# Row maxima handed over in two halves in both self-attentions, with the first pass of layer 0 begun earlier in the ring

## The reference

```
layer 0:  q, k, v = per-head layernorm(x @ W + b)
          scores = einsum('bqhd,bkhd->bhqk', q, k) * 16 ** -0.5
          probs  = softmax(scores, axis=-1)
          out    = einsum('bhqk,bkhd->bqhd', probs, v) @ Wo + bo
layer 1:  the same on q, k, v = x @ qkv_w + qkv_b, with a causal mask before the softmax
```

## Time and profile before

| | |
|---|---|
| median of 3 runs | 1895.42 us |
| profiled execution, time / span | 1903.1 / 1901.4 us |
| busy in the span: PE, DVE, ACT, POOL | 1543.4, 1226.4, 941.4, 515.6 us |
| mean granted clock of TensorE | 0.91 |
| L1113 (row maxima), 448 times | 481.2 us busy, 1107 ns each |
| L1045 (exponentials), 896 times | 440.1 us busy |
| L954, L993, L1005 on PE | 286.4, 272.4, 220.8 us busy |
| layer 0's attention, first fill to last output turned | 118.3 to 562.9 us |
| layer 1's first fill | 1132.1 us |

### The profile page before, as it was taken

How to read it: one execution, slowest core, us unless ns; L and a number is a source line. 1 busy time by engine, 2 the same in 40 slices (tenths; PEclk the granted TensorE clock), 3 DMA queues, 4 the chain that set the end, 5 groups by cost and what they waited for, 6 DMA issues and landing times. The chain is left out here.

```text
span 1901.4 us, 27565 instructions
## 1 busy us (share of the span) xinstructions
PE 1543.4 (81%) x8891; PEld 836.8 (44%) x8892; DVE 1226.4 (64%) x4679; ACT 941.4 (50%) x1856; POOL 515.6 (27%) x419
## 2 busy tenths in 40 slices
PE   5858999999973688888877767999987883369997
PEld 3511222222222566666666533333326672136664
DVE  6978887877505999999992446777725567501211
ACT  2823777777663555555544432666673652111211
POOL 1791000000001466555553150111211332240111
PEclk9956999999897899999987876999998996679999
DMA  6293334221010000000000186355402122531110
GB/s 210 82 210 58 45 47 99 41 41 18 26 32 13 1 2 1 1 1 1 1 2 1 34 232 89 46 69 111 90 3 88 15 40 36 202 106 36 45 45 8
DMA packets 112679, 106.01 MB, mean 56 GB/s; under 512 B 45523, under 2 KB 86555, under 8 KB 112542
## 3 DMA queue, kind: packets, MB, share of 16 engines
q1 hardware_dynamic: 107281, 93.83, 23.4%
q0 software_dynamic: 2640, 6.31, 0.9%
q10 hardware_dynamic: 2624, 4.19, 0.7%
HBM read 68.56 MB, written 36.41 MB: 55 GB/s over the span
## 5 line engine op out<-in xcount | busy, mean ns | idle before, releaser
L1113 DVE TENSOR_REDUCE arena<-banks 128x2 f32<-128x1024 f32 (+1 forms) x448 | 481.2, 1107 | 162.2 <-PE banks L954 105.6
L1045 ACT ACTIVATE arena<-banks 128x512 f32<-128x512 f32 (+3 forms) x896 | 440.1, 557 | 188.1 <-PE banks L993 181.5
L954 PE MATMUL banks<-arena 96*128 96x512 bf16 (+3 forms) x896 | 286.4, 397 | 55.3 <-DMA arena<-v 26.8
L993 PE MATMUL banks<-arena 98*128 98x512 bf16 (+3 forms) x896 | 272.4, 364 | 9.3 <-ACT arena L1045 6.8
L1005 PE MATMUL banks<-arena 128*32 128x512 f32 (+3 forms) x1792 | 220.8, 565 | 12.6 <-ACT arena L1045 6.5
L1712 DVE MATCH_REPLACE8 arena<-arena 128x77 f32<-128x77 f32 x1024 | 213.8, 223 | 0.0
L954 PEld LDWEIGHTS banks<-arena 96*128 96x128 bf16 x896 | 80.8, 102 | 238.3 <-DVE arena L1113 137.7
L993 PEld LDWEIGHTS banks<-arena 98*128 98x128 bf16 x896 | 82.5, 98 | 188.5 <-ACT arena L1045 124.4
L1602 POOL TENSOR_SCALAR arena<-arena 128x256 f32<-128x256 f32 x32 | 39.2, 1224 | 449.8 <-DVE arena L1689 449.8
L2498 DVE COPY arena<-banks 128x1024 f32<-128x1024 f32 x23 | 28.2, 1225 | 198.6 <-PE banks L2432 198.6
L1704 DVE MAX8 arena<-arena 128x8 f32<-128x77 f32 x1024 | 149.5, 224 | 0.9
(11 more groups left out here) (279 smaller groups left out, 2465.3 us busy)
## 6 DMA issues: line engine op xcount, KB each, us to landing
arena<-parts SPq DMA_DIRECT2D x192, 128.0 KB, 7.4
parts<-arena SPq DMA_DIRECT2D x24, 512.0 KB, 5.3
arena<-in_L_ffn_W SPq DMA_DIRECT2D x12, 1024.0 KB, 10.9
v<-arena SPq DMA_DIRECT2D x32, 256.0 KB, 2.3
arena<-v SPq DMA_DIRECT2D x16, 512.0 KB, 11.1
arena<-in_L_ffn_W ACTq DMA_DIRECT2D x4, 1024.0 KB, 9.4
arena<-sorted_rows SPq DMA_DIRECT2D x23, 129.0 KB, 2.2
arena<-sorted SPq DMA_DIRECT2D x23, 128.0 KB, 2.1
```

The source lines that it names most:

```text
L954: mm = pe.matmul(bank[:, 0:w], qst[r][0:KS, j, i * P:(i + 1) * P], kst[r][0:KS, j, kb * BANK:kb * BANK + w], start=True, stop=not diag)
L993: pe.matmul(bank, kst[r][0:KM, j, kt * P:(kt + 1) * P], qst[r][0:KM, j, half * BANK + lo:(half + 1) * BANK], start=True, stop=True).then_i ...
L1045: act.activation(prob[:, gi % 2 * G + j, lo:BANK], PS[:, 4 + n % 3, 0:BANK - lo], ACT.Exp, scale=SCALE).then_inc(sem(s + "_exp"), 1)
L1113: dve.tensor_reduce(m2[u % 2][:, 2 * pair:2 * pair + 2, i, kb], PS[:, 2 * (n % 2):2 * (n % 2) + 2, 0:w], AX.X, ALU.max).then_inc(sem(s + " ...
```

## The change

The maxima of a unit are handed over in two halves of 512 queries. DVE's three steps, PE's transpose, DVE's copy and the DMA now exist per half: 128x16 numbers each (32 rows after the transpose), and four DMAs, one per head, instead of one. Buffers `mh`, `mx` and `mT` are now indexed by the half, no longer by the unit's parity. PE's pass waits for the first half's rows at its start (`_rows0`) and for the second half's before the first group of the second half (`_rows1`).

The entries stand in the ring as follows: MAX of half 0 four fills after the last fill of that half, MAX of half 1 where MAX stood. In layer 0 (`not causal`) the deadlines also move: 24 fills instead of 40 come before the first pass, pass u carries the entries up to fill 28 of unit u+1, and in the passes of units 0 and 7 the entries up to that unit's second MAX are spread over the first quarter (`goal`, `early`). Layer 1 keeps its deadlines.

On SP, unit 2 is no longer loaded straight after unit 1: its 13 DMAs are issued after the row DMAs of unit 0. The waits of the following stages count one more ring entry per unit.

```diff
@@ -856,7 +856,7 @@
             R.at = SMALL_AT + SPARE
             m2 = [R.f32(G * TB * 2).rearrange("p (j t a) -> p j t a", j=G, a=2) for _ in range(2)]
             mx = [R.f32(G * TB).rearrange("p (j t) -> p j t", j=G) for _ in range(2)]
-            mh = [R.bf16(2 * G * TB) for _ in range(2)]
+            mh = [R.bf16(G * TB) for _ in range(2)]
             mT = [R.bf16(P) for _ in range(2)]
             rs = [R.f32(TB * G // 2).rearrange("p (t j) -> p t j", j=G) for _ in range(2)]
             osb = [out_area[:, half * BANK:(half + 1) * BANK] for half in range(2)]
@@ -867,8 +867,11 @@
             diagonal = [gi for gi, (half, kt, lo) in enumerate(groups) if causal and kt * P >= half * BANK]
             last_of = [max(i for i, g in enumerate(groups) if g[0] == half) for half in range(2)]
 
-            def hilo(u):
-                return mh[u % 2].rearrange("p (c j t) -> p c j t", c=2, j=G)
+            HT = TB // 2
+            HALF_FILLS = sum(1 for f in unit_fills if f[0] < HT)
+
+            def hilo(half):
+                return mh[half].rearrange("p (j c t) -> p c j t", c=2, j=G)
 
             PV_AT = G - 1 if causal else 1
             OUT_AT = G - 1 if causal else 2
@@ -877,11 +880,24 @@
             for u in range(NU):
                 feed += [(FILL, u, f) for f in range(NF)]
             for u in range(NU):
-                feed.insert(feed.index((FILL, u, NF - 1)) + (5 if u < NU - 1 else 1), (MAX, u, 0))
+                feed.insert(feed.index((FILL, u, HALF_FILLS - 1)) + 5, (MAX, u, 0))
+                feed.insert(feed.index((FILL, u, NF - 1)) + (5 if u < NU - 1 else 1), (MAX, u, 1))
+            first_due = feed.index((FILL, 1, AHEAD) if causal else (FILL, 0, 24))
             due = []
             for u in range(NU):
-                due.append(feed.index((FILL, u + 2, AHEAD)) if u + 2 < NU else len(feed))
-            first_due = feed.index((FILL, 1, AHEAD))
+                n, f = (u + 2, AHEAD) if causal else (u + 1, NF - 4)
+                due.append(feed.index((FILL, n, f)) if n < NU else len(feed))
+            early = 0.25
+
+            def goal(u, past):
+
+                at0 = due[u - 1] if u else first_due
+                if u in (0, NU - 1) and not causal:
+                    soon = max(at0, feed.index((MAX, u, 1)) + 1)
+                    if past <= early:
+                        return at0 + round((soon - at0) * past / early)
+                    return soon + round((due[u] - soon) * (past - early) / (1 - early))
+                return at0 + round((due[u] - at0) * past)
 
             def width(gi):
                 return BANK - groups[gi][2]
@@ -896,9 +912,9 @@
                 for gi in range(NGR):
                     for j in range(G):
                         past += width(gi) / G
-                        goal = at0 + round((due[u] - at0) * past / WORK)
-                        ring += feed[at:goal]
-                        at = goal
+                        upon = goal(u, past / WORK)
+                        ring += feed[at:upon]
+                        at = upon
                         if j == 2 and gi in (1, last_of[0] + 2):
                             half = 0 if gi > 1 else 1
                             if u or gi > 1:
@@ -913,14 +929,18 @@
             @block.sync
             def _(sp):
                 sp.wait_ge(sem(q + "_parts"), PARTS_ST)
-                for u in range(1, NST):
-                    load_unit(sp, l, u)
+                load_unit(sp, l, 1)
                 sp.wait_ge(sem(s + "_ones"), NST)
                 for u in range(NU):
 
-                    sp.wait_ge(sem(s + "_red"), entry[MAX, u, 0] + 1)
-                    sp.dma_start(qst[u % NST][KS:KM], mT[u % 2][0:2 * G * TB]).then_inc(sem(s + "_rows"), 16)
-                    if 1 <= u <= NU - NST:
+                    for half in range(2):
+                        sp.wait_ge(sem(s + "_red"), entry[MAX, u, half] + 1)
+                        for j in range(G):
+                            sp.dma_start(qst[u % NST][KS:KM, j, half * BANK:(half + 1) * BANK], mT[half][j * 2 * HT:(j + 1) * 2 * HT]
+                                         ).then_inc(sem(f"{s}_rows{half}"), 16)
+                    if u == 0:
+                        load_unit(sp, l, 2)
+                    elif u <= NU - NST:
                         sp.wait_ge(sem(s + "_pv"), u * NGR)
                         load_unit(sp, l, u - 1 + NST)
                     if l == 0 and u == 2:
@@ -957,9 +977,9 @@
                             mm = pe.matmul(bank[:, w - P:w], identb, future, start=False, stop=True)
                     mm.then_inc(sem(s + "_fill"), 1)
 
-                def turn_maxima(n, u):
-                    pe.wait_ge(sem(s + "_mh"), u + 1)
-                    pe.transpose(PS[0:2 * G * TB, 2 * (n % 2), 0:P // 2].bitcast(BF16), mh[u % 2], identb
+                def turn_maxima(n, u, half):
+                    pe.wait_ge(sem(s + "_mh"), 2 * u + half + 1)
+                    pe.transpose(PS[0:G * TB, 2 * (n % 2), 0:P // 2].bitcast(BF16), mh[half], identb
                                  ).then_inc(sem(s + "_fill"), 1)
 
                 def turn_output(n, u, half):
...
@@ -1013,8 +1033,11 @@
                 if l == 0:
                     pe.wait_ge(sem("xv"), 2 * B)
                 for u in range(NU):
-                    pe.wait_ge(sem(s + "_rows"), 16 * (u + 1))
+                    pe.wait_ge(sem(s + "_rows0"), 16 * G * (u + 1))
                     for gi in range(NGR):
+                        if gi == last_of[0] + 1:
+                            first_pass(upto[u][gi * G])
+                            pe.wait_ge(sem(s + "_rows1"), 16 * G * (u + 1))
                         for j in range(G):
                             first_pass(upto[u][gi * G + j])
                             second_pass(u, gi, j)
@@ -1083,18 +1106,22 @@
                     dve.memset(b.rearrange("p j t a -> p (j t a)"), LOWEST).then_inc(sem(s + "_m2"), 1)
                 dve.wait_ge(sem(s + "_m2"), 2)
 
-                def maximum(u):
-                    dve.wait_ge(sem(s + "_red"), entry[FILL, u, NF - 1] + 1)
-                    dve.tensor_tensor(mx[u % 2], m2[u % 2][:, :, :, 0], m2[u % 2][:, :, :, 1], ALU.max).then_inc(sem(s + "_mx"), 1)
-
-                def high(u):
-                    dve.wait_ge(sem(s + "_mx"), u + 1)
-                    dve.tensor_scalar(hilo(u)[:, 0], mx[u % 2], -1.0, None, ALU.mult).then_inc(sem(s + "_mhi"), 1)
-
-                def low(u):
-                    dve.wait_ge(sem(s + "_mhi"), u + 1)
-                    dve.scalar_tensor_tensor(out=hilo(u)[:, 1], in0=mx[u % 2], scalar=-1.0, in1=hilo(u)[:, 0], op0=ALU.mult,
-                                             op1=ALU.subtract).then_inc(sem(s + "_mh"), 1)
+                def maximum(u, half):
+                    dve.wait_ge(sem(s + "_red"), entry[FILL, u, (HALF_FILLS, NF)[half] - 1] + 1)
+                    t = slice(half * HT, (half + 1) * HT)
+                    dve.tensor_tensor(mx[half][:, :, 0:HT], m2[u % 2][:, :, t, 0], m2[u % 2][:, :, t, 1], ALU.max
+                                      ).then_inc(sem(s + "_mx"), 1)
+
+                def high(u, half):
+                    dve.wait_ge(sem(s + "_mx"), 2 * u + half + 1)
+                    dve.tensor_scalar(hilo(half)[:, 0], mx[half][:, :, 0:HT], -1.0, None, ALU.mult).then_inc(sem(s + "_mhi"), 1)
+
+                def low(u, half):
+                    dve.wait_ge(sem(s + "_mhi"), 2 * u + half + 1)
+                    dve.scalar_tensor_tensor(out=hilo(half)[:, 1], in0=mx[half][:, :, 0:HT], scalar=-1.0, in1=hilo(half)[:, 0],
+                                             op0=ALU.mult, op1=ALU.subtract).then_inc(sem(s + "_mh"), 1)
+
+                steps = (maximum, high, low)
 
                 def normalize(u, half, n):
                     pair, a = u // 2, u % 2
@@ -1112,20 +1139,17 @@
                         i, kb, pair, w = unit_fills[f]
                         dve.tensor_reduce(m2[u % 2][:, 2 * pair:2 * pair + 2, i, kb], PS[:, 2 * (n % 2):2 * (n % 2) + 2, 0:w],
                                           AX.X, ALU.max).then_inc(sem(s + "_red"), 1)
-                        if f == 0 and u:
-                            maximum(u - 1)
-                        elif f == 1 and u:
-                            high(u - 1)
-                        elif f == 2 and u:
-                            low(u - 1)
+                        if f < len(steps) and u:
+                            steps[f](u - 1, 1)
+                        elif 0 <= f - HALF_FILLS < len(steps):
+                            steps[f - HALF_FILLS](u, 0)
                         elif (u, f) == (NU - 1, NF - 1):
-                            maximum(u)
-                            high(u)
-                            low(u)
+                            for step in steps:
+                                step(u, 1)
                     elif kind == MAX:
-                        if u >= 2:
```

(13 more changed lines are left out.)

## The result

The changed kernel takes 1889.85 us (median of 14 runs) against 1897.04 us for the kernel before (14 runs): a ratio of 0.9961 (95% interval 0.9948 to 0.9975), some 7 us faster. The forecast was 1875.5 us with 1867 to 1886. The sign was right, the size a third of it.

The account below looks back on a forecast made before the run. DVE was taken to bound layer 0's lead-in, PE its full passes, ACT and bank turnover the last. Layer 0's -15.7 and layer 1's -4.2 us made -19.9, taking 1895.4 to 1875.5 us; range 1867 to 1886.

Parts of the forecast that it names:

- a MAX costs 0.25: Self-attention passes: each added MAX entry lengthens a pass by 0.25 us, read from one group (2.68 against 2.84).
- steps 5 and layer 1: Six more MAX in layer 0's passes 1 to 6, +1.5 us; seven more in layer 1, +1.8 us.
- The wait I named: Layer 1 before pass 0: PE's 5.98 us wait for rows queued behind unit 2's load goes, -6.0 us.
- The lead-in by number of fills: Layer 0 before pass 0: 16 fewer fills at 1.179 us each start the pass 18.9 us earlier.
- No wait for the rows at any pass: Rows land in time at pass starts; the rival giving back 1.4 us at each of 14 had chance 0.04.
- The stall at pass 7: Layer 0, start of pass 7: row wait of 2.12 us and half-speed clock go, -5.8 us.
- Pass 0: Layer 0's pass 0 carries 36 fills instead of 32 and was forecast about 3.3 us longer.
- the 2.4 us of its row: Time from the row copy's end to hand-over at pass 7, used to forecast rows landing before layer 0's pass 0.
- The extra cost of the hand-overs: Rival, both layers: extra hand-overs cost more than air, gain about 12 us, 1883 us; chance 0.16.
- upper bound of 4 us a layer: Added edits in each attention: 0 to 0.5 us per pass, 0 to 4 us per layer.
- The clock did not stay low through pass 0: Rival, layer 0: low clock through pass 0 at half speed, 1911 us, slower; chance 0.04.
- Layer 1's wait did not stay: Rival: layer 1 keeps its row wait, its rows still behind unit 1's load; gain 14, 1881 us; chance 0.08.

Follow-up runs that it names:

- experiments 3 and 4: The second: kernel before, layer 0 with seven useless MAX entries, 1902.22 us; or with DVE's three steps repeated uselessly, 1898.66 us. The first: see experiment 3.
- experiment 3: Changed kernel with layer 0's maxima in halves but the old deadlines, layer 1 as in the kernel before: 1903.12 us, ratio 1.0022.
- experiment 1: Kernel before with one edit: SP issues unit 2's load after unit 0's row DMA, maxima still whole: 1890.38 us, ratio 0.9965.
- Experiment 6: Changed kernel with layer 1's last MAX issued two matmuls into pass 7: 1883.92 us, ratio 0.9922; also the changed kernel traced again unedited.

## Why the prediction was wrong

**The step that failed is the price of a MAX** ("a MAX costs 0.25", steps 5 and layer 1). I read it off one group in which the MAX stood where a fill had been left out (2.68 against 2.84 us). The fill that made room stands elsewhere in the pass: the trace of before already has a group of three fills and 3.68 us, which I did not count. And I took the order of the fills as given, though one entry more moves it. The runs put a further MAX at 1.19 to 1.21 us a pass (experiments 3 and 4), nearly all of it in groups without a MAX. Five passes at 1.53 instead of 0.3 are 6.1 of the 6.5 us missing in layer 0; the rest is that the last of the five was 0.4 us shorter than the others before. The other 0.34 of the 1.53 came with the new deadlines: they put the MAX into a group of two fills (3.68 us), where experiment 3 has one of three fills (3.68) and one of a fill and the MAX (2.67). That is 0.17 us a half.

**Layer 1.** The wait I named was the queue behind unit 2's load, and it went (experiment 1 shows it alone). The halves cost 0.57 us a pass where I took 0.25. The last MAX, one slot closer to the last fill, added 1.1 us of wait and in this trace the low clock; I had not looked at that place. Experiment 6 shows both: without them the end of the layer takes 74.7 us, before 75.1. Part of this was bad luck, since the clock stayed low for 10 us here, 3 us or not at all in other traces.

**What held.** The lead-in by number of fills (-18.6 for -18.9). No wait for the rows at any pass. The stall at pass 7 gone. Pass 0 came out 1.1 us better than forecast, by a clock that came up sooner. That is in part luck: in four traces of this same layer 0 it came 2.7 to 5.0 us after the first L1013, and at the output turn in the middle of pass 0 the latest stood 0.5 us behind the earliest. The section of the Trainium skill that the forecast cites for a DMA's fixed cost ("DMA: Bandwidth & Descriptors", section "Anatomy of one DMA") is written for DMAs that GpSimd issues; the rows go out on SP, so the step rests on the 2.4 us of its row alone.

**The rivals.** The extra cost of the hand-overs was among them (1883 us, 0.16) and was what happened, but at its upper bound of 4 us a layer it was still too small: layer 0 paid 8.1 in five passes. I had bounded it by PE waits seen in the brackets, when the trace already had groups of 3.68. The clock did not stay low through pass 0, and no L1013 waits for a DMA in the whole trace. Layer 1's wait did not stay.

## What to carry to other kernels

- In a ring of two places, a small entry costs what it does to the large ones, not what it runs. A 0.24 us transpose cost 1.2 us a pass where rounding spread the entries, since it moved the fills of half a pass into dearer slots; with the slots held it cost 1.06, over half of it a fill that waited for the one just issued. Price it from a whole period with one entry more, never from the one group it stands in.
- An early issue of a load that nobody needs yet is not free: a 16 KB DMA behind it held PE for 6 us. Moving one line on SP gave 6.5 us, where the whole change gave 7.2.
- When an order is spread by rounding, compare the position of the last entries before and after; one slot nearer to its producer cost 1.1 us more of wait, and in three traces of four the clock fell behind it.

## What the runs showed of the hardware

- A PE wait of 1.7 us inside a dense stretch was followed by 1.2 GHz in three traces of four, for about 3 us in two of them and 10 in one, with the same order of work. In the nine traces with a wait of 0.57 us or none at that MAX the clock stayed up.
- After DVE-bound work at 1.2 GHz (PE 86% busy in the trace before), the full clock came some 3 us after the first matmul of pass 0 in the changed kernel's trace and about 7 us in the trace before; 2.7 to 5.0 us over four traces of one order. The Trainium skill ("TensorE: Matmul & The Clock Gate", section "The HAM clock gate") says that activity releases the low clock; both traces agree, and the delays show that a forecast can't rely on one of them.
